# A routed expert layer on one core: gates in DRAM rows of their own, h stored in sixteen half batches, the first part in another order

## The reference

```python
h = (x - mu) * jax.lax.rsqrt(var + 1e-05) * ln_g + ln_b
m_t = h.mean(1, keepdims=True)
v_t = h.var(1, keepdims=True)
h_norm = (h - m_t) * jax.lax.rsqrt(v_t + 1e-08)
...
gamma = jax.nn.softplus(gamma) + 1e-08
h = h_norm * gamma[:, None, :] + beta[:, None, :]
h_flat = h.reshape(-1, D)
probs = jax.nn.softmax(h_flat @ router_w, axis=-1)
gates, idx = jax.lax.top_k(probs, TOPK)
gates = gates / gates.sum(-1, keepdims=True)
combine = jnp.zeros((N, E), h_flat.dtype).at[jnp.arange(N)[:, None], idx].add(gates)
hid = jax.nn.relu(jnp.einsum('nd,edf->nef', h_flat, exp_w1) + exp_b1)
eout = jnp.einsum('nef,efd->ned', hid, exp_w2) + exp_b2
y = jnp.einsum('ned,ne->nd', eout, combine)
return x + y.reshape(x.shape)
```

## Time and profile before

| | |
|---|---|
| median of 3 runs | 495.33 us (493.65 to 496.61) |
| the profiled execution | 495.07 us |
| its span in the profile | 493.1 us |
| busy share: PE, DVE, ACT, POOL | 92%, 78%, 56%, 46% |
| mean granted TensorE clock | 0.971 |
| scatters and gathers on POOL | 71 each, mean 1.72 and 1.17 us |

### The profile page before, as it was taken

How to read it: one execution, slowest core, us unless ns; L and a number is a source line. 1 busy time by engine, 2 the same in 40 slices (tenths; PEclk the granted TensorE clock), 3 DMA queues, 4 the chain that set the end, 5 groups by cost and what they waited for, 6 DMA issues and landing times.

```text
span 493.1 us, 15848 instructions
## 1 busy us (share of the span) xinstructions
PE 453.9 (92%) x5696; PEld 414.9 (84%) x5696; DVE 383.5 (78%) x1440; ACT 278.0 (56%) x840; POOL 225.0 (46%) x183
## 2 busy tenths in 40 slices
PE   7958748999999999999999999999999999999990
PEld 5744437899999899999999999999899999999990
DVE  4988858899888878878888888888888877777640
ACT  2558526566665666655566565566566555555440
POOL 0850121444554554555555454554555544444422
PEclk9689979999999999999999999999999999999996
DMA  8952673444444434434444443444443332322321
GB/s 317 414 178 86 170 237 119 88 99 109 89 88 94 93 87 99 110 87 90 92 94 92 115 90 89 94 92 97 104 96 88 48 54 47 56 45 47 49 30 22
DMA packets 37820, 51.68 MB, mean 105 GB/s; under 512 B 8064, under 2 KB 29840, under 8 KB 37488
## 3 DMA queue, kind: packets, MB, share of 16 engines
q0 software_dynamic: 13632, 18.91, 22.4%
q1 hardware_dynamic: 21488, 31.14, 19.8%
q10 hardware_dynamic: 2624, 0.62, 0.5%
HBM read 36.74 MB, written 18.11 MB: 111 GB/s over the span
## 4 chain that ended last, share of the span: by engine, by line
PE 79%; DVE 7%; DMA 5%; ACT 3%; issue 2%; POOL 1%; SPq 1%; ACTq 0%; DVEq 0%; POOLq 0%
PE bank L700 37%; PE bank L707 35%; PE bank L655 3%; DMA out_rows<-yout,tok 2%; PE bank L649 2%; DVE bns L773 1%; DMA par<-in_params 1%; DMA h_rows<-wlo 1%; PE bank L519 1%; PE bank L531 1%; DVE tns L797 1%; DVE wlo L1160 1%; ACT hid L465 1%; DVE hidlo L1175 1%; DMA hg<-h_rows,tok 1%
## 5 line engine op out<-in xcount | busy, mean ns | idle before, releaser
L465 ACT ACTIVATE hid<-bank,par 128x128 f32<-128x128 f32 x568 | 162.8, 369 | 163.8 <-PE bank L700 161.0
L700 PE MATMUL bank<-hThi,whi 128*128 128x128 f16 x1136 | 188.9, 220 | 5.4 <-issue 1.7
L700 PE MATMUL bank<-hTlo,whi 128*128 128x128 f16 x1136 | 188.8, 220 | 0.0
L330 POOL DMA_INDIRECT out_rows<-yout,tok x71 | 122.3, 1722 | 111.3 <-ACT yout L477 91.5
L700 PE MATMUL bank<-hThi,wlo 128*128 128x128 f16 x1136 | 156.8, 220 | 0.0
L707 PE MATMUL bank<-wlo,hidhi 128*128 (+1 forms) x568 | 154.8, 273 | 0.0
L707 PE MATMUL bank<-whi,hidlo 128*128 (+1 forms) x568 | 154.8, 273 | 0.0
L707 PE MATMUL bank<-whi,hidhi 128*128 (+1 forms) x568 | 154.8, 273 | 0.0
L322 POOL DMA_INDIRECT hg<-h_rows,tok x71 | 83.1, 1170 | 113.2 <-DVE tok L1151 92.4
L700 PEld LDWEIGHTS bank<-hThi,whi 128*128 (+1 forms) x1136 | 111.2, 98 | 15.2 <-issue 7.1
L700 PEld LDWEIGHTS bank<-hTlo,whi 128*128 (+1 forms) x1136 | 111.6, 98 | 5.5
(11 more groups left out here) (171 smaller groups left out, 444.0 us busy)
## 6 DMA issues: line engine op xcount, KB each, us to landing
stage<-in_exp_w SPq DMA_DIRECT2D x64, 256.0 KB, 3.0
whi<-in_x SPq DMA_DIRECT2D x8, 512.0 KB, 8.4
out_rows<-in_x SPq DMA_DIRECT2D x8, 512.0 KB, 15.8
h_rows<-wlo SPq DMA_DIRECT2D x8, 512.0 KB, 4.0
hg<-h_rows,tok POOLq DMA_INDIRECT x71
out_rows<-yout,tok POOLq DMA_INDIRECT x71
b2row<-in_exp_b SPq DMA_DIRECT2D x1, 1024.0 KB, 20.4
par<-in_params SPq DMA_DIRECT2D x1, 517.5 KB, 6.2
```

The costliest lines, as they stand in the source:

```text
L330: gp.indirect_dma_start(out=out, out_offset=bass.IndirectOffsetOnAxis(ap=tok[:, t:t + 1], axis=0), in_=yout[:, t % 2, :], in_offset=None, ...
L465: ins = S(hid32[:, par, c * P:(c + 1) * P], bk_hid[half][:, (c - 4 * half) * P:(c - 4 * half + 1) * P], ACT.Relu, bias=vcol[:, bass.ds(e * ...
L700: hid_ins = MM(o, lhs[w, k], h[:, par, k * P:(k + 1) * P], start=(n == 0), stop=(n == 3 * KD - 1))
```

## The change

Gates get a table of their own, `gate_rows`, filled by one transfer of ScalarE, and rows of h are 256 numbers wide. SP stores h by halves of a batch, sixteen transfers, each as soon as its half_rows is done, and no gates. POOL gathers gates for each tile in an indirect transfer of its own, and VectorE waits for it. The orders of VectorE, ScalarE and TensorE in the first part are new, chunks 4 and 5 are split ahead of the loop, 6 and 7 in tile 0, and chunks 4 to 7 all wait for gather 0.

```diff
-    h_dram = nc.dram_tensor("h_rows", (ROWS, HROW), F32).ap()
+    h_dram = nc.dram_tensor("h_rows", (ROWS, D), F32).ap()
+    g_dram = nc.dram_tensor("gate_rows", (ROWS, E), F32).ap()
...
-            return banks[5] if i >= BP * 2 and i % 2 == 1 else banks[7]
+            return banks[5] if i >= BP and i % 2 == 1 else banks[7]
...
             if t < 3:
-                return range(4 + 2 * t, 6 + 2 * t)
+                return ((6, 7), (), (8, 9))[t]
             return range(7 + t, min(8 + t, CHUNKS))
...
-            for b in range(6):
-                store_h(b)
-            sp_.wait_ge(s_comb, 1)
-            for b in range(BP):
-                store_gates(sp_, b)
-            for b in range(6, B):
-                store_h(b)
+            for b in range(B):
+                for g in range(2):
+                    half = slice(g * JB * D // 2, (g + 1) * JB * D // 2)
+                    sp_.wait_ge(s_hrow, 2 * b + g + 1)
+                    sp_.dma_start(h_v[b][:, half], hrow[b][:, half]).then_inc(s_hst, 16)
...
+            sp_.wait_ge(s_gh[0], 16)
             for i in range(4, 8):
-                if i % 2 == 0:
-                    sp_.wait_ge(s_gh[i // 2 - 2], 16)
                 load_chunk(i)
...
+            def gather_gates(t):
+                gp.wait_ge(s_tok, t + 1)
+                if t >= NHG:
+                    gp.wait_ge(s_gate, t - NHG + 1)
+                gp.indirect_dma_start(out=gt[:, t % NHG, :], out_offset=None, in_=g_dram,
+                                      in_offset=bass.IndirectOffsetOnAxis(ap=tok[:, t:t + 1], axis=0)).then_inc(s_gg[t % NHG], 16)
...
-            gp.wait_ge(s_hst, 16 * B)
-            gp.wait_ge(s_spare, 16 * 4)
-            gp.wait_ge(s_combst, 16 * B)
+            gp.wait_ge(s_spare, 16 * 6)
+            gp.wait_ge(s_hst, 16 * 2 * B)
             for t in range(3):
                 gather(t)
+            gp.wait_ge(s_combst, 16)
+            for t in range(2):
+                gather_gates(t)
...
                 if t >= 2:
                     scatter(t - 2)
+                if t + 2 < TILES:
+                    gather_gates(t + 2)
                 if t + 3 < TILES:
                     gather(t + 3)
...
+            time_deviation(1)
             half_rows(0, 0)
-            half_rows(0, 1)
-            time_deviation(1)
-            half_rows(1, 0)
             modulate(2)
             modulate(3)
-            half_rows(1, 1)
+            half_rows(0, 1)
             time_deviation(2)
-            half_rows(2, 0)
             modulate(4)
-            copy_logits(0)
             modulate(5)
             time_deviation(3)
+            copy_logits(0)
+            half_rows(1, 0)
+            modulate(6)
+            half_rows(1, 1)
...
-            for b in range(BP, B):
-                store_gates(act, b)
+            act.dma_start(comb_v, comb.rearrange("p (b n) -> p b n", b=B)).then_inc(s_combst, 16)
...
             slot_table(2, 0)
             warm(6, 1)
+            warm(12, 1)
             tile_transpose(0)
...
-            ve.wait_ge(s_par, 16)
-            V.tensor_tensor(g2[:, :], g_k, g_k, ALU.mult).then_inc(s_g2, 1)
             stats(0)
-            moments(0, stats(1))
...
             def gate(t, e):
-                V.tensor_copy(gates[:, t:t + 1], hg[:, t % NHG, bass.ds(e + D, 1)]).then_inc(s_gate, 1)
+                ve.wait_ge(s_gg[t % NHG], 16 * (t // NHG + 1))
+                V.tensor_copy(gates[:, t:t + 1], gt[:, t % NHG, bass.ds(e, 1)]).then_inc(s_gate, 1)
```

More of the change, by code:

```diff
@@ L483, in _ @@
             tile_hi(0, 0)
+            for i in range(4, 6):
+                w_hi(i)
             es = [first[0]] * 6
@@ L597, in _ @@
             transposes(4, 1)
[L598 to L600 removed]
+            back(0, 0)
+            back(0, 1)
             transposes(5, 0)
             transposes(5, 1)
[L603 to L604 removed]
             transposes(6, 0)
```

152 lines of the change are left out of this document (70 added, 82 removed).

## The result

| | before | changed |
|---|---|---|
| median (range), us | 495.58 (493.65 to 498.70, 20 runs) | 498.27 (496.59 to 499.82, 20 runs) |
| ratio to before, 95% interval | | 1.0043 [1.0023, 1.0063] |
| profiled execution, its span | 495.07, 493.1 | 499.43, 497.6 |

What follows compares the result with a forecast made beforehand. TensorE was taken to bound the tile loop, so only the time before it could gain: +0.2 - 3.0 (first product) - 2.0 (clock, earlier splits) = -4.8 us on 495.07, 490.3; predicted median 490.5, range 487.5 to 494.3.

Steps and rivals of the forecast that it cites:

- The last scatters are unchanged: 0.: End of the loop: the final scatters stay as before, so they add 0 us.
- the first tiles' -2.0: From the first product into the first tiles: higher clock and earlier weight splits gain 2.0 us.
- Front, +0.2: Up to the selection: the earlier statistics' lead is all lost to waits, so both_chosen(1) comes 0.2 us later.
- From selection to first product, -3.0: Between selection and first expert product: earlier stores and gather 0 gain 3.0 us; first product at 68.5 instead of 71.31.
- the weights bound this now: Before the first product: the weights, not the gather, come last, with the first product at 68.5.
- the gates landed at 70.8, so this hides: First tiles: tile 0's gates, issued at 67.8, land 3.0 us later, hidden by VectorE splitting chunks until 70.7.
- The higher clock: First product on: TensorE, idle 1.9 us instead of 5, runs at 2.4 GHz, saving 1.9 us.
- Loop, 0: Tile loop: the added gates' gather, taken as 1.2 us a tile, fits POOL's idle time and costs 0.
- Rival (d): Loop: POOL becomes the bound, a tile 0.11 us over, 7.5 us for 68 tiles: 498 us; chance 0.07.
- Rival (c): Stores of h aren't earlier; first product moves under 1 us, gain about 1.5: 494 us; chance 0.17.
- rival (b): First tiles give less through half clock and a 2.6 us register load; gain 2 to 3: 493 us; chance 0.10.

Runs made afterwards that it cites:

- run 13: The kernel before with 71 more indirect gathers on GpSimd, one a tile, into a tile that nothing reads: 498.67 us, ratio 1.0044.
- run 7: The changed kernel without GpSimd's drain at the end: 490.69 us, ratio 0.9886.
- run 8: The kernel before without GpSimd's drain at the end: 492.89 us, ratio 0.993.
- Run 15: The changed kernel without GpSimd's end drain, gates gathered behind each tile's rows, new order around the router, plus 18 and 8 warm products: 487.77 us.
- runs 9, 6: The changed kernel with five more GpSimd drains in the loop (505.5 us, one execution), and with one more there (496.54 us, ratio 0.9994), respectively.
- run 5: The changed kernel with 63 more indirect gathers on GpSimd from tile 8 on, whose data nothing uses: 500.67 us, ratio 1.0081.
- Run 11: The changed kernel without GpSimd's end drain, gates of tiles 0 and 1 gathered right behind their own tile's rows: 489.55 us, ratio 0.9834.
- run 12: The kernel before with only the changed data layout (tables, stores, gathers, chunk waits), old order, without GpSimd's end drain: 493.44 us, ratio 0.9924.
- run 4: The changed kernel with VectorE's copy of a tile's gate moved from the middle to the end of the iteration: 497.98 us, ratio 1.0039.

## Why the prediction was wrong

**Two steps failed. The one that made a loss of it is the last term of the loop: "The last scatters are unchanged: 0."** They are, but behind them stands GpSimd's drain, 2.65 us longer after a third gather a tile (run 13, without the change's edits; runs 7 and 8 without the drain). That is more than the whole loss of 2.1 us by the ratio. The row was in the trace of before, 4.32 us long, and I read the tail only as far as the last scatter.

**The rest of the sum was too large, above all the first tiles' -2.0.** Taking the drain's 2.65 from the loss by the ratio leaves a gain of 0.5 us; runs 7 and 8, which have no drain, differ by 0.65 in their spans (2.2 in their times, see there). So the rest is worth about half a microsecond by these two, and 2.2 if run 8's time is taken as it stands, where 4.8 were forecast. By its terms:

- *Front, +0.2.* Measured +3.1 in the result's profile against that of before. Over all profiles nothing so large is seen: three of the old program average 57.35 at the selection (55.03, 57.41, 59.60), five of the changed one 57.35 (56.11 to 58.17). So whether the term was right is open; that it was worked out from one good execution of before is a fault of its own. The mechanism is the one named, a wait for the exponential behind rows of h. In the result's profile VectorE's gap was forecast to end at 50.6 and ended at 53.5, and there the clock was mis-sized (logits(4, 6) took 3.04 us, not 1.9, after a wait of 1.95) and modulate(7), 43.05 where 42.0 was forecast. Run 15, which keeps the clock up, has the selection at 55.6.
- *From selection to first product, -3.0.* Measured -3.57, with the last half landed and the token numbers last to be waited for, as forecast; half a batch took 2.6 us to land in the median, 3.0 forecast. (What the prediction cites for 2.6, the Trainium skill, DMA: Bandwidth & Descriptors, section Anatomy of one DMA — SWDGE (gpsimd) path, is stated for transfers that GpSimd issues, and SP issues these.) Its parts missed and made up for each other: from the selection to gather 0 it took 7.8 us where 7.15 were forecast, its rows 3.5 where 3.05 were, and "the weights bound this now" was wrong, for they were split 11.2 us after the selection, forecast 12.15, and the gathered rows came last. That the term came out near is in part luck.
- *First tiles, -2.0.* Measured +2.2 in the result's profile (first product -0.4, tile 8 +1.8) and -0.1 in run 7's (-0.46, -0.53). From the first product to tile 8's transposition it takes 31.9 us in the profiles of before and of run 8, and 34.1, 33.9, 33.7, 31.8 and 31.7 in the result, runs 9, 6, 7 and 5: about +1 in the mean and in none near -2.0. The step "the gates landed at 70.8, so this hides" failed: 6.5 us in place of 3.0 in the result. VectorE waited 1.80, 1.07, 1.11, 0.43 and 0 us for them in those five, and the three with over 1 us are the three that lost 1.8 to 2.2. TensorE's clock fell in the same three (to 0.50 to 0.64) and not in the other two, so how that loss is split between the wait and the clock isn't separated. I had taken the landing time from a row with fewer bytes beside it (DMA share 0.77 at 66 to 68 us and 0.28 at 68 to 70; 1.01 where the gates were under way). Run 11 takes VectorE's wait away, and TensorE still stands 1.90 us for the weights. The higher clock, on which 1.9 of the 2.0 rested, came for the first product. It was lost again in the next wait in the result; where it stayed, in runs 7 and 5, these tiles took 0.1 and 0.2 us less than before and not 2.0, so the pace of TensorE by itself didn't give the gain.
- *Loop, 0.* Right: 99.29% against 99.31, a gates' gather of 1.02 us where 1.2 were taken. Rival (d) is refuted for this kernel; run 5 shows that it starts with a fourth transfer, not the third. The stretching of POOL's instructions that the rule of the Trainium skill (SBUF — State Buffer, section SBUF: two separate sides) would give didn't come: 1.02 and 1.00 us with VectorE 83% busy.

Rival (c) is refuted by the stores, rival (b) happened in part, and the one that decided wasn't in the list. What stays open: what sets a drain to 4.3 or to 7.0 us, how what the change is worth apart from it is split, and why run 12 gained only 5.0 us of its drain's 6.96.

## What to carry to other kernels

Read the profile to its last row: what each engine does between its last work and the end is paid in full, and an added stream of GpSimd's indirect transfers can lengthen it. If every one of its transfers has been waited for, GpSimd's drain at the end can go, which gave 4.7 us and 7.6 by the spans (3.3 and 7.6 by the times). Profile the kernel before more than once: its selection moved by 4.6 us between three executions, about as much as the whole gain forecast. Take the time of a transfer from a row with the traffic that it will meet after the change, and issue the small one that somebody waits for ahead of the burst. Where TensorE waits two microseconds or more, reckon with half clock behind it (it fell in some executions and not in others), and ask first whether TensorE is what bounds that stretch.

## What I had not expected of the hardware

- GpSimd's drain at the end takes 4.3 to 7.0 us with all transfers landed, and isn't monotone in their number: 4.32 after 142, 6.96 and 6.93 after 213, 4.88 after 276; five in one loop took 4.58 to 6.77, and the one ahead of all transfers 0.19.
- Executions of the same instructions up to tile 8, there up to 3.9 us apart (101.08 in run 5, 105.01 in the result), differ in whether TensorE's clock fell after a wait: it did after 3.39 us, not after 1.90 (run 7) or 1.67 (run 5), and did after 1.95 in run 4.
- A gather of 32 bytes a row takes GpSimd as long as one of 1,024 bytes (1.02 and 1.00 us), and its rows alone, without the gates, took 1.00 where they took 1.20 with them.
